# Eight pieces of work change their place in the engines' order, in a two-layer graph network with attention

## The reference

```
xn = layernorm(x)
x = x + relational_gnn(xn, edges, types) + linear_attention(xn)   # layer 0
x = x + routed_feed_forward(layernorm(x))                         # trees of leaves k, q, v, f, with softmax attention
xn = layernorm(x)
x = x + gcn(xn, edges) + linear_attention(xn)                     # layer 1
x = x + shared_and_expert_feed_forward(layernorm(x))
```

## Time and profile before

| what | value |
|---|---|
| three runs | 2495.48, 2498.00, 2500.18 us; median 2498.0 |
| profiled execution, its own time | 2490.95 us |
| its span, first to last instruction | 2488.8 us |
| mean granted TensorE clock | 0.985 |
| busy: TensorE / weight load / VectorE / ScalarE / GpSimd | 2373.5 / 1917.6 / 1418.6 / 852.1 / 236.1 us |
| share of the span | 95 / 77 / 57 / 34 / 9 % |
| chain of work that ended last | PE 81%, DVE 9%, DMA 4%, issue 3%, ACT 2% |
| DMA | 405.99 MB, mean 163 GB/s |

### The profile page before, as it was taken

How to read it: one execution, slowest core, us unless ns; L and a number is a source line. 1 busy time by engine, 2 the same in 40 slices (tenths; PEclk the granted TensorE clock), 3 DMA queues, 4 the chain that set the end, 5 groups by cost and what they waited for, 6 DMA issues and landing times.

```text
span 2488.8 us, 31259 instructions
## 1 busy us (share of the span) xinstructions
PE 2373.5 (95%) x12005; PEld 1917.6 (77%) x12005; DVE 1418.6 (57%) x2478; ACT 852.1 (34%) x1055; POOL 236.1 (9%) x238
## 2 busy tenths in 40 slices
PE   6999999999999999989989999999989999999998
PEld 5788987777777777877867777878757779877665
DVE  6886443233333333345778896756874333558876
ACT  4222331121111212122157776632744122133542
POOL 1101320000000000011111111100111010202000
PEclk9999999999999999999999999999999999999999
DMA  5345823432132322133688999875975422254884
GB/s 147 89 110 132 163 81 113 122 102 74 54 93 60 93 60 68 55 116 124 241 269 316 345 347 307 270 236 163 338 261 157 119 76 68 84 177 162 302 283 147
DMA packets 167675, 405.99 MB, mean 163 GB/s; under 512 B 69327, under 2 KB 69616, under 8 KB 167498
## 3 DMA queue, kind: packets, MB, share of 16 engines
q1 hardware_dynamic: 144284, 340.48, 42.4%
q0 software_dynamic: 17440, 49.29, 6.9%
q10 hardware_dynamic: 5774, 13.81, 2.0%
HBM read 359.44 MB, written 56.76 MB: 167 GB/s over the span
## 4 chain that ended last, share of the span: by engine, by line
PE 81%; DVE 9%; DMA 4%; issue 3%; ACT 2%; DVEq 0%; SPq 0%; ACTq 0%; POOL 0%; POOLq 0%
PE PS L308 17%; PE PS L309 16%; PE PS L310 16%; PE PS L1203 7%; PE PS L979 4%; PE PS L581 3%; PE PS L1493 2%; PE PS L1876 2%; DVE low L300 2%; PE PS L1883 2%; PE PS L1885 2%; PE PS L1884 2%; PE PS L2353 1%; PE PS L327 1%; PE PS L3264 1%
## 5 line engine op out<-in xcount | busy, mean ns | idle before, releaser
L300 DVE TENSOR_TENSOR low<-raw,high 128x1024 fp32r<-128x1024 f32 x473 | 570.6, 1244 | 116.0 <-ACT high L288 113.1
L288 ACT ACTIVATE high<-raw 128x1024 fp32r<-128x1024 f32 x476 | 484.3, 1056 | 308.5 <-PE PS L310 239.0
L308 PE MATMUL PS<-high,xt_high 128*125 128x512 f32 x1280 | 517.2, 404 | 18.9 <-DVE low L300 7.9
L309 PE MATMUL PS<-low,xt_high 128*125 128x512 f32 x1280 | 510.4, 399 | 0.0
L310 PE MATMUL PS<-high,xt_low 128*125 128x512 f32 x1280 | 508.6, 397 | 0.0
L308 PEld LDWEIGHTS PS<-high,xt_high 128*125 128x125 f32 x1280 | 240.6, 188 | 82.1 <-issue 9.2
L310 PEld LDWEIGHTS PS<-high,xt_low 128*125 128x125 f32 x1280 | 240.2, 188 | 62.2
L309 PEld LDWEIGHTS PS<-low,xt_high 128*125 128x125 f32 x1280 | 240.5, 188 | 57.5 <-issue 0.2
L1227 ACT ACTIVATE y_high<-PS 125x512 fp32r<-125x512 f32 x80 | 47.8, 598 | 507.8 <-PE PS L310 507.8
L1238 DVE TENSOR_TENSOR y_low<-PS,y_high 125x512 fp32r<-125x512 f32 x80 | 55.3, 691 | 291.5 <-ACT y_high L1227 291.5
L1203 PE MATMUL PS<-y_high,a_kind 125*125 125x512 f32 x400 | 158.4, 396 | 0.0
(11 more groups left out here) (548 smaller groups left out, 3860.7 us busy)
## 6 DMA issues: line engine op xcount, KB each, us to landing
raw<-in_L_ffn_ew SPq DMA_DIRECT2D x96, 512.0 KB
raw<-in_L_gnn_weight SPq DMA_DIRECT2D x64, 512.0 KB
raw<-in_L_ffn_k_w SPq DMA_DIRECT2D x64, 512.0 KB, 6.0
raw<-in_L_ffn_q_w SPq DMA_DIRECT2D x64, 512.0 KB
raw<-in_L_ffn_v_w SPq DMA_DIRECT2D x64, 512.0 KB
raw<-in_L_ffn_f_w SPq DMA_DIRECT2D x64, 512.0 KB, 8.1
adjacency<-a_stage SPq DMA_DIRECT2D x10, 1120.0 KB
a_kind<-adjacency POOLq DMA_DIRECT2D x8, 1367.2 KB, 8.5
```

The source lines that it names most:

```text
L288: a.e.activation(high_of(i)[:, 0:w], RAW[PLACE_OF[i]][:, 0:w], ACT.Copy).then_inc(*a.step(part_high, 1, [("high", i)]))
L300: v.e.tensor_tensor(LOW[p][:, 0:w], RAW[p][:, 0:w], high_of(i)[:, 0:w], ALU.subtract).then_inc(*v.step(signal, 1, [("low", i)]))
L308: p.e.matmul(dst, xh[:, kt, xs], wh[:, c], start=first and j == 0, stop=False)
L309: p.e.matmul(dst, xh[:, kt, xs], wl[:, c], start=False, stop=False)
```

## The change

Eight pieces of work stand at another place of their engine's list; nothing is computed otherwise. (1) In `start_tensor` tile 2 is turned before the last part of fills 0 and 1. (2) In both attentions the last head tile is turned after output tile 0; the waits of output tiles 0 and 1 go down to the first half of the heads' division, and ScalarE and VectorE split the parts of the first output half (and one more) right after the queries. (3) In layer 0, on the last output tile, 2 instead of 4 parts are split, and the first relation tile waits for output tile 8 only. (4) The degree sums stand after the splits of gate tiles 0 and 1, the roots after the last aggregate. (5) On gate tile 4 of the first half two parts are split. (6) In both `total`s of layer 1 VectorE's split for the tile that follows stands before the last sum. (7) On tile 4 of the second GNN half three parts are split, and the first keys' tile of the second half stands before the sums, on TensorE, ScalarE (before the fifth row load) and VectorE. (8) The memset of the values' ones stands after the keys.

```
 start_tensor:
         for j, part in enumerate(Wk[0]):
+            if j == 3:
+                turn(2)
             for n in range(2):
...
-        turn(2)
         turn(3)
 M0 = mixer_buffers("L0_mix", P1 + 20480, Wq, Wo, (4, 2))      # m.more
 M1 = mixer_buffers("L1_mix", P1 + 20480, Wq1, Wo1, (4, 4))
 mixer_tensor:
-        turn(4)
         for h in range(2):
             for t in range(TT):
                 n = TT * h + t
-                p.wait_ge(at("xl", m.p, t), at("o out", m.p, n - 4) if n > 3 else at("heads out", m.p, 4, 1))
+                p.wait_ge(at("xl", m.p, t), at("o out", m.p, n - 4) if n > 3 else at("heads out", m.p, 4, n // 2))
                 rows_tile(p, t, m.wo[h], m.OH, m.OL, n % 4, "o", m.p, n)
+                if n == 0:
+                    turn(4)
                 head_rows(p, h, t)
 mixer_scalar, after the queries:
+        high_parts(a, ahead(a, m.wo[0][0], 0))
 mixer_vector, after the queries and before the key-value mask:
+        low_parts(v, ahead(v, m.wo[0][0], 0))
 both, over the output tiles:
-                low_parts(v, ahead(v, m.wo[h][0], t, 4 if t == TT - 1 else 1))
+                low_parts(v, ahead(v, m.wo[h][0], t, m.more[h] if t == TT - 1 else 1))
 make_y_tensor:
-        p.wait_ge(at("yl", n - 3) if n > 2 else at("o out", "L0_mix", 9))
+        p.wait_ge(at("yl", n - 3) if n > 2 else at("o out", "L0_mix", 9 if n else 8))
 relations_vector:
-                if n == 79:
-                    degrees_vector(v)
 gate_to:
-        return ahead(x, Wgate[h][top][0], t)
+        return ahead(x, Wgate[h][top][0], t, 2 if (h, t, top) == (0, 4, 0) else 1)
 gates_vector:
         low_parts(v, gate_to(v, 0, 1, 0))
+        degree_sums_vector(v)
         aggregate_vector(v, 15)
+        degree_roots_vector(v)
 graph_tensor:
         for t in range(TT):
             gnn(1, t)
+        keys(1, [0])
         total(1)
-        keys(1)
+        keys(1, range(1, TT))
 graph_scalar:
-            high_parts(a, ahead(a, Wgnn[h][0], t))
+            high_parts(a, ahead(a, Wgnn[h][0], t, 3 if h and t == TT - 1 else 1))
...
-        back(1)
-        keys(1)
+        back(1, range(TT - 1))
+        keys(1, [0])
+        back(1, [TT - 1])
+        keys(1, range(1, TT))
 graph_vector, gnn:
-            low_parts(v, ahead(v, Wgnn[h][0], t))
+            if (h, t) != (1, 0):
+                low_parts(v, ahead(v, Wgnn[h][0], t, 3 if h and t == TT - 1 else 1))
 graph_vector, keys:
-                low_parts(v, ahead(v, Wk1[h][0], t))
+                if (h, t) != (1, 1):
+                    low_parts(v, ahead(v, Wk1[h][0], t))
 graph_vector, total:
+                if j == TT - 1:
+                    low_parts(v, ahead(v, Wk1[1][0], 1) if h else ahead(v, Wgnn[1][0], 0))
                 v.wait_ge(at("sum", h, j), at("x2 back", h, j))
 graph_vector:
+        keys(1, [0])
         total(1)
+        keys(1, range(1, TT))
         v.wait_ge(v.last, *[at("acc1 stored", 1, j) for j in range(TT)])
         e.memset(VN[:, :, :, 128:130], 1.0).then_inc(*v.mark("ones v1"))
-        keys(1)
```

More of the change, by code:

```diff
@@ L942, in program, with mixer_buffers @@
         pass
-    def mixer_buffers(p, base, wq, wo):
+    def mixer_buffers(p, base, wq, wo, more):
         m = Mixer()
-        m.p, m.wq, m.wo = p, wq, wo
+        m.p, m.wq, m.wo, m.more = p, wq, wo, more
         m.QT = place(f"q_cols_{p}", [128, 8, NP], F32, base + 20800)
@@ L956, in mixer_buffers @@
         return m
-    M0 = mixer_buffers("L0_mix", P1 + 20480, Wq, Wo)
+    M0 = mixer_buffers("L0_mix", P1 + 20480, Wq, Wo, (4, 2))
     AO_BANK = (6, 4, 6, 4, 4)
@@ L1034, in mixer_scalar @@
             for t in range(TT):
-                high_parts(a, ahead(a, m.wo[h][0], t, 4 if t == TT - 1 else 1))
+                high_parts(a, ahead(a, m.wo[h][0], t, m.more[h] if t == TT - 1 else 1))
                 out_rows(a, h, t)
@@ L1254, in add_kind, with degree_sums_vector, degree_roots_vector @@
             v.e.tensor_copy(ASUM[:, m, :], a).then_inc(*v.mark("kinds", r, m))
-    def degrees_vector(v):
+    def degree_sums_vector(v):
         v.e.tensor_reduce(deg[:, :], ASUM[:, :, :], axis=AX.X, op=ALU.add).then_inc(*v.mark("degree sums"))
+    def degree_roots_vector(v):
         v.wait_ge(v.last)
@@ L2794, in program @@
     BV1 = place("bias_v1", [PT, D], F32, R0 + 97472)
-    M1 = mixer_buffers("L1_mix", P1 + 20480, Wq1, Wo1)
+    M1 = mixer_buffers("L1_mix", P1 + 20480, Wq1, Wo1, (4, 4))
     def f_stored():
@@ L2832, in gnn_half, with keys @@
                 ins.then_inc(*p.mark("gnn", t))
-        def keys(h):
-            for t in range(TT):
+        def keys(h, ts=range(TT)):
+            for t in ts:
                 n = TT * h + t
@@ L2908, in keys, with back @@
                 key_features_scalar(a, KN[:, t, 512 * h:512 * h + 512], TMP[t % 2][:, :], at("k1 out", n), None if before is None else at("k1 rows", before), "k1 parts", n)
-        def back(h):
-            for j in range(TT):
+        def back(h, js=range(TT)):
+            for j in js:
                 w = SG[j % 4]
```

## The result

The changed kernel takes 2463.9 us (median of 4 runs, 2461.70 to 2466.56) against 2497.7 us before (4 runs). The ratio is 0.9867, 95% interval 0.9853 to 0.9881: 33.8 us faster. The forecast was 2466.6, 31.4 us by its sum. In a second series on one chip it was 2461.07 against 2498.42, ratio 0.9847 (0.9829 to 0.9865). One execution of the kernel before, in a later series, took 3367 us at a granted clock of 0.652; it is left out everywhere as a slow state of the chip.

A forecast was written before the change was run, and what follows sets the result against it. It took TensorE, busy 95% of the span, as the bound. Nine terms sum to 31.4 us, taking 2490.95 to 2459.6; as the profiled execution lay 7 us below the median, it forecast 2466.6, range 2457 to 2480.

The forecast's parts named there:

- Step 1: Start: turning tile 2 of x before the last quarter of the first two key tiles gains 2.6 us.
- Steps 2 and 9: Attention heads: turning the last head tile behind output tile 0 gains 3.7 us in layer 0, 2.3 in layer 1.
- Step 3: Hand-over to the relations: waiting for tile 8 only, with two splits there, gains 6.6 us, of which 2.5 is clock.
- Steps 4 and 5: Gates: splits before the degree sums gain 5.2 us, two splits on gate tile 4 gain 3.1.
- Steps 6 to 8: Layer 1's graph stage: splits before last sum 2.3 us, keys' tile before second sums 4.3, remaining keys' parts split 1.3.
- The moved clock: Rival, whole kernel: the clock's losses, 7.1 us of the sum, move instead of going; 2473.7 us, chance 0.13.
- The weight stream: Rival, routed layers: their weight stream paces the kernel and absorbs the earlier 21.2 us; 2487.8 us, chance 0.05.
- the new wait: Rival: a late first sum or low delta tile gives back 3 to 5 us; about 2471 us, chance 0.09.

The follow-up runs named there:

- keys_tile_one_split: The changed kernel, but tile 4 of the second GNN half splits 1 part instead of 3; 2470.26 us.
- graph_part_alone: The kernel before with only the three functions of layer 1's graph stage changed; 2488.04 us, ratio 0.9957.
- the busy stall: The kernel before with 17 unread full-size products issued in TensorE's 4.05 us stall before the relations; 2496.59 us, ratio 0.9998.
- without_graph_part: The changed kernel with the three functions of layer 1's graph stage as before; 2473.95 us, ratio 0.9897.
- after_again: The changed kernel once more, nothing altered, beside the others on one chip; 2461.07 us, ratio 0.9847.

## Why the prediction was right, by its steps

- The bound was read right. Nine of TensorE's stalls were named, each with the instruction that stood ahead of the late one; eight are gone and the ninth, at the start, is 1.52 us (1.4 forecast). Two of the signs came out as well: the mean granted clock rose from 0.985 to 0.987 in the profiled pair (0.003 forecast), and the idle time fell by 22 us (22 to 25 forecast).
- Step 1 was mis-sized: 2.6 forecast (with 0 to 2.5 more for the clock left open), 4.9 measured. The chain gave 2.2 (37.07 to 34.86) or, with the first product's own shift of 0.3, 2.5; the rest is the clock, for which I counted nothing. Late turning has 12 to 14 slow products behind its stall in each of four profiles, the early one has none behind its stall of about 1.5 us in any. The turning itself waits for its rows between nothing and 2.6 us, by how many of the very first products ran slow; in keys_tile_one_split, where it waited 2.64 us, there are 8 or 9 slow products behind the turning and the later stall is gone.
- Steps 2 and 9: 3.7 and 2.3 forecast, 3.7 and 2.1 to 4.1 measured. The loosened wait is 1.05 of each. The two larger figures of layer 1 are 8 slow products behind the same stall in one profile and a stall of 1.50 us for a low part in the other. The 2.4 us of splits put after the queries are hidden, as said: the heads' stage starts no later. What these splits are worth could not be tried alone: without them output tile 0 wants a part that ScalarE splits behind the high half of head tile 4, which is turned only after output tile 0, so by the code no engine could go on.
- Step 3: 6.6 forecast, 6.8 against the profile it was made from, 5.3 against the other. I used both edits; the shorter wait alone gives all of it, the postponed splits alone all but 0.94 us. The unread products separated stall and clock: the clock's share, 2.5 forecast, is 2.6 us by the profile of before and 1.4 by graph_part_alone. That the forecast met the first so well is partly luck: it was read from that very execution.
- Steps 4 and 5: 5.2 + 3.1 = 8.3 forecast, 8.34 measured against the profile of before. The reduction and the roots are hidden with 3.7 us to spare.
- Steps 6 to 8: 7.9 forecast; 7.2 to 8.3 against the profile of before, more against the two others. The three splits that I had priced at 0.8 us of delay are the condition of the whole step.
- The rivals. The moved clock is refuted: the mean granted clock is 0.981 to 0.985 in the executions of the kernel before and 0.987 to 0.990 in the nine of the changed one. The matmuls of 0.60 us or more in length number 154, 183 and 160 in the profiles of the kernel before, with the busy stall and with the graph part alone, and 129 and 123 in the two of the changed kernel: 25 to 60 fewer, at 0.195 us each 5 to 12 us by estimate, where the sum had 7.1. The weight stream and the new wait are refuted by the stages above. A wait of 0.75 us before the last sum of the first half in the profile after is none of the change's: without_graph_part, whose graph functions are those of before, has it with 0.51 us, and after_again has none.
- What I had no step for: single executions differ by up to 5.7 us in the routed layers, 4.3 in the edges stage and 4.6 behind layer 1's attention. The profiled pair, which I would have compared first, is wrong by 9 us about the gain.

The Trainium skill's rule from the prediction (the free-running watch on activity, TensorE: Matmul & The Clock Gate, "The HAM clock gate") agrees with the traces here: the stall of 2.92 us has 10 slow products behind it in one kernel and none in another, and the unfilled stall at the hand-over 13 in one execution and 6 in another. The rival drawn from it, that the slow products would only move elsewhere, did not come about: there are fewer of them.

## What to carry to other kernels

Where a matrix engine is 95% busy, list its stalls, take for each the queue of the engine that ended it, and ask what in that queue isn't needed yet: here a reduction, a statistics chain, splits for a later group. A moved piece of work covers a stall only if its own inputs are made before the same late queue; check that before the move. Compare stages between profiles, not profiled totals, and expect a range for the clock's share: here a removed stall of 2.4 to 4.3 us was worth between its idle time and twice that. Where two edits guard one place, try each alone: here either would have done most of it.

## What the runs showed of the hardware

- The clock after a stall. The granted clock was 0.54 for 6 us behind 4.05 us of idle time and 1.00 when the same time was filled with products that nobody reads: standing still cost 2.6 us on top, and 1.4 in another execution with 3.81 us of idle time at the same place (6 slow products instead of 13). A stall of 4.3 us at the start had 12 to 14 slow products behind it in four profiles; one of 2.92 us had none in one kernel and about 10 with a turning in another, at the same place of the same instruction order. Of the unchanged first products at 18 us, 8 to 11 ran slow in some profiles and hardly any in others.
- A DMA issue costs ScalarE's queue 0.3 to 0.7 us, and eight of them 3.8 us from 1943.48 to 1947.3 in the kernel without the splits; a split behind them waits as behind a long instruction.
